# Partial sums of the middle stages: transfers that add in DRAM instead of load, add and store

## The reference

```python
lora_delta = lora_B @ lora_A * 0.5
normalized = (weight + lora_delta) / scale          # groups of 128
w_eff = codebook[searchsorted(thresholds, normalized)] * scale + lora_delta
h   = x @ w_eff.T                                   # 4096 x 2048
out = x_in + h @ W_base.T + b_base + 2 * mixture(h @ A_w.T, softmax(h @ router_w.T), cores) @ B_w.T
```

## Time and profile before

| | |
|---|---|
| median of 3 runs | 2330.87 us (2330.3 to 2331.73) |
| profiled execution: time, span | 2334.6 us, 2331.3 us |
| PE busy | 2252.6 us (97%) |
| DVE, ACT, POOL busy | 1952.5 (84%), 1495.4 (64%), 1391.5 us (60%) |
| HBM read, written | 306.41 MB, 151.13 MB |
| token part of stage 1, of stage 2 | about 891 to 1244 us, about 1427 to 1776 us |

### The profile page before, as it was taken

How to read it: one execution, slowest core, us unless ns; L and a number is a source line. 1 busy time by engine, 2 the same in 40 slices (tenths; PEclk the granted TensorE clock), 3 DMA queues, 4 the chain that set the end, 5 groups by cost and what they waited for, 6 DMA issues and landing times.

```text
span 2331.3 us, 31903 instructions
## 1 busy us (share of the span) xinstructions
PE 2252.6 (97%) x11610; PEld 2061.2 (88%) x11610; DVE 1952.5 (84%) x2501; ACT 1495.4 (64%) x1962; POOL 1391.5 (60%) x902
## 2 busy tenths in 40 slices
PE   3989899999999999999999999999999999999999
PEld 2445479999999989999999989999999999999998
DVE  8999998889988977989997988999996766777676
ACT  7999978989877764666664865666663664121221
POOL 6888846669874545878775635988872132233331
PEclk9999999999999999999999999999999999999999
DMA  6787854444334334656664334566656666656454
GB/s 209 260 288 272 315 208 170 163 170 145 133 128 149 116 109 169 254 214 240 248 231 153 115 109 167 221 244 246 234 223 195 187 193 192 226 192 235 189 222 154
DMA packets 133233, 459.62 MB, mean 197 GB/s; under 512 B 14114, under 2 KB 66914, under 8 KB 96354
## 3 DMA queue, kind: packets, MB, share of 16 engines
q1 hardware_dynamic: 133076, 457.59, 56.1%
HBM read 306.41 MB, written 151.13 MB: 196 GB/s over the span
## 4 chain that ended last, share of the span: by engine, by line
PE 80%; DVE 8%; DMA 4%; ACT 3%; POOL 2%; issue 2%; SPq 0%; DVEq 0%; POOLq 0%; ACTq 0%
PE m L1228 6%; PE m L1227 6%; PE m L1229 6%; PE m L1179 5%; PE m L1180 5%; PE m L1181 5%; DVE acc L1701 5%; PE m L1120 5%; PE m L1334 4%; PE m L1336 4%; PE m L1335 4%; PE m L1294 3%; PE m L1293 3%; PE m L1295 3%; PE m L1284 3%; PE m L1285 2%
## 5 line engine op out<-in xcount | busy, mean ns | idle before, releaser
L1701 DVE SCALAR_TENSOR_TENSOR acc<-mk,dj,acc 128x1024 f32<-128x1024 uint8 x736 | 944.4, 1283 | 91.4 <-ACT mk L1449 73.2
L1449 ACT ACTIVATE mk<-wr,bj 128x1024 uint8<-128x1024 f32 x736 | 811.1, 1139 | 0.5 <-DVE acc L1701 0.4
L2014 POOL TENSOR_TENSOR pp<-pp,tm 128x1024 f32<-128x1024 f32 x184 | 456.9, 2483 | 22.9 <-POOL tm L2000 1.5
L2000 POOL TENSOR_SCALAR tm<-mp,dj 128x1024 f32<-128x1024 uint8 x192 | 225.8, 1177 | 219.8 <-ACT mp L1455 213.0
L1799 DVE TENSOR_TENSOR kl<-kw,kh 128x416 fp32r<-128x416 f32 (+3 forms) x310 | 240.5, 785 | 84.5 <-ACT kh L1484 83.5
L1484 ACT ACTIVATE kh<-kw 128x416 fp32r<-128x416 f32 (+3 forms) x310 | 169.1, 548 | 183.2 <-DMA kw<-in_wb 91.9
L1228 PE MATMUL m<-gl,xh 128*128 128x384 f32 (+2 forms) x800 | 280.9, 351 | 0.0
L1227 PE MATMUL m<-gh,xh 128*128 128x384 f32 (+2 forms) x800 | 280.6, 351 | 0.0
L1229 PE MATMUL m<-gh,xl 128*128 128x384 f32 (+2 forms) x800 | 279.9, 350 | 0.0
L1455 ACT ACTIVATE mp<-wr,bj 128x1024 uint8<-128x1024 f32 x224 | 255.0, 1139 | 13.7 <-POOL wr L1980 13.7
L1761 DVE TENSOR_TENSOR part<-m,part 128x448 f32<-128x448 f32 (+4 forms) x362 | 210.8, 593 | 34.1 <-PE m L1229 16.7
(11 more groups left out here) (249 smaller groups left out, 5140.8 us busy)
## 6 DMA issues: line engine op xcount, KB each, us to landing
part<-part SPq DMA_DIRECT2D x191, 1036.0 KB, 4.8
rows<-in_wb SPq DMA_DIRECT2D x61, 1036.0 KB, 4.8
out<-part SPq DMA_DIRECT2D x31, 1024.0 KB, 4.8
kw<-in_ws SPq DMA_DIRECT2D x128, 208.0 KB, 2.7
xw<-in_x SPq DMA_DIRECT2D x96, 256.0 KB, 5.1
kw<-in_wb SPq DMA_DIRECT2D x92, 192.0 KB, 2.4
wr<-in_w SPq DMA_DIRECT2D x32, 512.0 KB, 5.8
dl<-delta SPq DMA_DIRECT2D x30, 512.0 KB, 5.4
```

What stands on the lines that cost most here:

```text
L1449: e.activation(R.mk[m % NM], w, ACT.Identity, bias=R.bj[:, j:j + 1], scale=GROW).then_inc(S["mk"], 1)
L1701: e.scalar_tensor_tensor(R.acc, R.mk[m % NM], R.dj[:, j:j + 1], R.acc, ALU.mult, ALU.add).then_inc(S["ac"], 1)
L2014: e.tensor_tensor(R.pp, first, R.tm[scaled_level(q, i)], ALU.add).then_inc(S["pp"], 1)
```

## The change

In stages 1 and 2 the part is no longer loaded. Each unit is evicted by a copy into the part buffer (products that come second add to the first in SBUF, as before), and the whole buffer is then added to `part` in DRAM by one transfer that POOL issues, `add_part`, with `accum_op=ALU.add` and each row of 2072 cut in two pieces of 1036. The evictions are divided: ACT copies the rests and the chunks 0 to 2 (`mul_copied`, semaphore `ea`), DVE the seven products and chunks 3 and 4 (`mul_evicted`, semaphore `ed`). The first write to a buffer waits for the transfer that added it three tokens before (new semaphores `pa`). The event `half_stored` stands after unit 10 of a mixed pair (6 of a pair of chunks) for its even token, `pair_stored` at unit 1 of the next pair for its odd token, and `close` for token 31. The transfer of a token in stage 2 waits for that of stage 1. SP keeps the x loads, the weight loads and the part stores of stage 0. The first ring pieces of the next weight part wait for `pa` instead of `po`.

```diff
...
@@ -221,3 +221,2 @@
                 yield ("x_split", g, 2 * p + 3)
-                yield ("more", g, p)
             if at == 4 and mixed(p + 1):
@@ -236,2 +235,6 @@
                 yield ("split", SPLITS[g + 1][at])
+        if at == (10 if mixed(p) else 6):
+            yield ("half_stored", g, p)
+        if p and at == 1:
+            yield ("pair_stored", g, p - 1)
         if at == (9 if mixed(p) else 5):
@@ -578,6 +581,20 @@
 PAIR_FIRST = {g: {p: min(k for k, u in enumerate(UNITS_OF[g]) if u[0] == p) for p in range(PAIRS)} for g in MIXED}
-MC_BASE, ED_BASE = [0, NCH * NT], [0, len(DVE_CHUNKS) * NT]
+
+
+def by_scalar(u):
+
+    return u[1] == "rest" or u[1] == "chunk" and u[3] in ACT_CHUNKS
+
+
+MC_BASE, EA_BASE, ED_BASE = [0, NCH * NT], [0, len(ACT_CHUNKS) * NT], [0, len(DVE_CHUNKS) * NT]
 for _g in MIXED:
+    scalar_units = sum(by_scalar(u) for u in UNITS_OF[_g])
     MC_BASE.append(MC_BASE[-1] + len(UNITS_OF[_g]))
-    ED_BASE.append(ED_BASE[-1] + len(UNITS_OF[_g]))
+    EA_BASE.append(EA_BASE[-1] + scalar_units)
+    ED_BASE.append(ED_BASE[-1] + len(UNITS_OF[_g]) - scalar_units)
+
+
+def token_units(g, t, scalar):
+
+    return [k for k, u in enumerate(UNITS_OF[g]) if u[0] == t // 2 and t % 2 in unit_tokens(u)[0] and by_scalar(u) == scalar]
 
...
@@ -602,4 +614,12 @@
 
-def added(g, k):
-    return ED_BASE[g] + k + 1
+def evicted(g, k):
+
+    scalar = by_scalar(UNITS_OF[g][k])
+    earlier = sum(by_scalar(u) == scalar for u in UNITS_OF[g][:k])
+    return ("ea", EA_BASE[g] + earlier + 1) if scalar else ("ed", ED_BASE[g] + earlier + 1)
+
+
+def wait_unit_evicted(e, S, g, k):
+    name, count = evicted(g, k)
+    e.wait_ge(S[name], count)
 
@@ -664,3 +684,3 @@
     if g in MIXED:
-        e.wait_ge(S["ed"], added(g, PAIR_FIRST[g][t // 2] + NCH * (t % 2) + c))
+        wait_unit_evicted(e, S, g, PAIR_FIRST[g][t // 2] + NCH * (t % 2) + c)
     elif c in ACT_CHUNKS:
@@ -864,3 +884,6 @@
             p = HOME[r]
-            e.wait_ge(S[f"po{p}"], 16 * (g * PER_SLOT[p] + (g == LAST and p == (NT - 1) % 3)))
+            if g == 1:
+                e.wait_ge(S[f"po{p}"], 16 * PER_SLOT[p])
+            else:
+                e.wait_ge(S[f"pa{p}"], 16 * (g - 1) * PER_SLOT[p])
         if g == LAST:
@@ -884,19 +907,6 @@
 
-    def load_part(g, t):
-        if t < 3:
-            e.wait_ge(S["used"], NS * (g - 1) + RELEASED[t])
-        else:
-            e.wait_ge(S[f"po{t % 3}"], slot_round(g, t - 3))
-        e.dma_start(R.part[t % 3], part[t]).then_inc(S[f"pi{t % 3}"], 16)
-
-    def store_part(g, t):
-        if g == 0:
-            for c in range(NCH):
-                wait_evacuated(e, S, g, t, c)
-        else:
-            e.wait_ge(S["ed"], added(g, last_unit(g, t, 0)))
-        if (g, t) == (LAST - 1, NT - 1):
-            e.dma_start(part[t][:, 0:HX], R.part[t % 3][:, 0:HX]).then_inc(S[f"po{t % 3}"], 16)
-        else:
-            e.dma_start(part[t], R.part[t % 3]).then_inc(S[f"po{t % 3}"], 16)
+    def store_part(t):
+        for c in range(NCH):
+            wait_evacuated(e, S, 0, t, c)
+        e.dma_start(part[t], R.part[t % 3]).then_inc(S[f"po{t % 3}"], 16)
 
...
@@ -1015,8 +1021,2 @@
                 load_x(g, 1)
-            if s == NS - 5:
-                load_part(g, 0)
-            if s == NS - 3:
-                load_part(g, 1)
-            if s == NS - 1:
-                load_part(g, 2)
         elif what == "chunk":
...
@@ -1038,14 +1038,4 @@
                 load_x(g, 2 * p + 3)
-            if p:
-                store_part(g, 2 * p - 1)
-        elif what == "more":
-            g, p = at
-            if p:
-                load_part(g, 2 * p + 2)
         elif what == "half_done":
-            g, p = at
-            store_part(g, 2 * p)
-            if p + 1 < PAIRS:
-                load_part(g, 2 * p + 3)
-            elif g == 1:
+            if at == (1, PAIRS - 1):
                 raw(2 * FIRST[LAST])
...
@@ -1523,2 +1513,15 @@
         e.activation(R.part[t % 3][:, cols(c)], R.m[c][:, 0:width(c)], ACT.Copy).then_inc(S["ea"], 1)
+
+    def mul_copied(g, k):
+        p, kind, u, i = UNITS_OF[g][k]
+        t = 2 * p + u
+        part, bank = R.part[t % 3], (*R.m, R.pd)[unit_bank(UNITS_OF[g][k])]
+        if t >= 3 and k == token_units(g, t, True)[0]:
+            e.wait_ge(S[f"pa{t % 3}"], slot_round(g - 1, t - 3))
+        e.wait_ge(S["mc"], multiplied(g, k))
+        if kind == "chunk":
+            to, of = part[:, cols(i)], bank[:, 0:width(i)]
+        else:
+            to, of = rest_columns(part, i), rest_bank(bank, i)
+        e.activation(to, of, ACT.Copy).then_inc(S["ea"], 1)
 
@@ -1626,2 +1629,6 @@
                 weight(g + 1, 1)
+        elif what == "mul":
+            g, k = at
+            if k and by_scalar(UNITS_OF[g][k - 1]):
+                mul_copied(g, k - 1)
         elif what == "next_rounded":
@@ -1742,3 +1749,3 @@
 
-    def mul_added(g, k):
+    def mul_evicted(g, k):
         p, kind, *at = UNITS_OF[g][k]
@@ -1746,16 +1753,15 @@
         part, bank = R.part[t % 3], (*R.m, R.pd)[unit_bank(UNITS_OF[g][k])]
-        if k == first_unit(g, t, 0):
-            e.wait_ge(S[f"pi{t % 3}"], slot_round(g - 1, t))
+        if t >= 3 and k == token_units(g, t, False)[0]:
+            e.wait_ge(S[f"pa{t % 3}"], slot_round(g - 1, t - 3))
         e.wait_ge(S["mc"], multiplied(g, k))
         if kind == "chunk":
-            c = at[1]
-            to, of = part[:, cols(c)], bank[:, 0:width(c)]
-        elif kind == "rest":
-            to, of = rest_columns(part, at[1]), rest_bank(bank, at[1])
-        else:
-            first = HX * TARGET[at[0]][1]
-            to, of = part[:, first:first + SW], bank[:, 0:SW]
-            before = target_before(g, k)
-            if before is not None:
-                e.wait_ge(S["ed"], added(g, before))
+            e.tensor_copy(part[:, cols(at[1])], bank[:, 0:width(at[1])]).then_inc(S["ed"], 1)
+            return
+        first = HX * TARGET[at[0]][1]
+        to, of = part[:, first:first + SW], bank[:, 0:SW]
+        before = target_before(g, k)
+        if before is None:
+            e.tensor_copy(to, of).then_inc(S["ed"], 1)
+            return
+        wait_unit_evicted(e, S, g, before)
         e.tensor_tensor(to, of, to, ALU.add).then_inc(S["ed"], 1)
...
@@ -2061,2 +2068,11 @@
         e.tensor_tensor(s4, a12, s2, ALU.subtract).then_inc(S["qs"], 1)
+
+    def add_part(g, t):
+        wait_unit_evicted(e, S, g, token_units(g, t, True)[-1])
+        wait_unit_evicted(e, S, g, token_units(g, t, False)[-1])
+        if g == 1:
+            e.wait_ge(S[f"po{t % 3}"], 16 * PER_SLOT[t % 3])
+        else:
+            e.wait_ge(S[f"pa{t % 3}"], slot_round(g - 2, t))
+        e.dma_start(part[t], R.part[t % 3], accum_op=ALU.add, max_dma_last_dim=4 * HX).then_inc(S[f"pa{t % 3}"], 16)
 
@@ -2163,3 +2179,9 @@
             token_sums(*at)
+        elif what == "half_stored":
+            add_part(at[0], 2 * at[1])
+        elif what == "pair_stored":
+            add_part(at[0], 2 * at[1] + 1)
         elif what == "close":
+            if at[0]:
+                add_part(at[0], NT - 1)
             if at[0] == 1:
...
```

More of the change, by code:

```diff
@@ L105 @@
     "sl", "lb0", "lb1", "lb2", "la0", "cb", "id", "la", "ds0", "ds1", "ds2", "dq0", "dq1", *(f"w{r}" for r in range(RAW)), "r0", "r1", "r2", "f2", "f3", "f5", "f6", "f7",
-    *(f"k{r}" for r in range(RING)), "x0", "x1", "x2", "x3", "pi0", "pi1", "pi2", "po0", "po1", "po2",
+    *(f"k{r}" for r in range(RING)), "x0", "x1", "x2", "x3", "pa0", "pa1", "pa2", "po0", "po1", "po2",
     *(f"pj{k}" for k in range(5)), *(f"ou{k}" for k in range(5)), "xs0", "xs1", "bw", "bb", "cr",
@@ L578 @@
 PAIR_FIRST = {g: {p: min(k for k, u in enumerate(UNITS_OF[g]) if u[0] == p) for p in range(PAIRS)} for g in MIXED}
-MC_BASE, ED_BASE = [0, NCH * NT], [0, len(DVE_CHUNKS) * NT]
+def by_scalar(u):
+    return u[1] == "rest" or u[1] == "chunk" and u[3] in ACT_CHUNKS
+MC_BASE, EA_BASE, ED_BASE = [0, NCH * NT], [0, len(ACT_CHUNKS) * NT], [0, len(DVE_CHUNKS) * NT]
 for _g in MIXED:
+    scalar_units = sum(by_scalar(u) for u in UNITS_OF[_g])
     MC_BASE.append(MC_BASE[-1] + len(UNITS_OF[_g]))
-    ED_BASE.append(ED_BASE[-1] + len(UNITS_OF[_g]))
+    EA_BASE.append(EA_BASE[-1] + scalar_units)
+    ED_BASE.append(ED_BASE[-1] + len(UNITS_OF[_g]) - scalar_units)
+def token_units(g, t, scalar):
+    return [k for k, u in enumerate(UNITS_OF[g]) if u[0] == t // 2 and t % 2 in unit_tokens(u)[0] and by_scalar(u) == scalar]
 def last_unit(g, t, reads):
     return max(k for k, u in enumerate(UNITS_OF[g]) if u[0] == t // 2 and t % 2 in unit_tokens(u)[reads])
-def first_unit(g, t, reads):
-    return min(k for k, u in enumerate(UNITS_OF[g]) if u[0] == t // 2 and t % 2 in unit_tokens(u)[reads])
 def prod_unit(g, p, n):
@@ L1001, in sync_program @@
             if g == LAST:
-                if s == 1:
-                    store_part(LAST - 1, NT - 1)
-                if s == 4:
```

(10 more changed lines are left out.)

8 lines of the change are left out of this document (4 added, 4 removed).

## The result

The changed kernel takes 2365.29 us (median of 4, 2364.13 to 2365.82) against 2330.59 us for the kernel before on the same chip: 1.0152 times as long, 95% interval 1.0139 to 1.0164. Forecast were 2328.0 us and a range from 2320 to 2350. The profiled execution took 2364.13 us with a span of 2362.3 us, 31.0 us above the span of before.

A forecast was written before the change was run, and what follows sets the result against it. PE bounds the two token stages, busy 343.72 of 348.35 us. Terms -4.8 - 1.0 + 2.5 + 0.5 = -2.8 us against the median of 2330.87 gave 2328.0 us, range 2320 to 2350.

The forecast's parts named there:

- The stage starts: Start of both token stages: DVE freed of the first two chunks' evictions, 1.0 us gained, between 0 and 2.3.
- POOL trails PE by about that much: Middle of stages: transfers' waits on evictions cost nothing more, as POOL runs about 5.9 us behind, read at 1085.17 us.
- 1.4 + 8 us plus POOL's trail of 5 is below 18: Middle of stages: issue, landing and trail fit the buffer's some 15 us plus 3 in the bank, so DVE doesn't wait.
- the booked -4.8: Middle of both stages: 4.8 of about 6 us of PE's losses gained as DVE's lateness goes, between 0 and 6.
- The term put at nothing: POOL's queue: 32 transfers a stage at 1.4 us fit its idle time, 20.0 of 21.2 us a pair, costing nothing.
- +2.5 and +0.5 us: Stage ends: later transfers delay next weights, 2.5 us lost at the first (0 to 8), 0.5 at the second (to 6).
- into an emptier queue: First stage's end: weight loads go out 5.1 us later but take 2.4 us, reaching ACT 0.8 us later than before.
- the rival of the slow transfer: Adding transfer of about 12 us or more costs at stage ends and in the middle: 2339 us, chance 0.13.
- POOL as the bound: Rival: from 2.0 us a transfer POOL is as long as PE in every pair; at 2.4, 2352 us; chance 0.26.
- the 7 us that I had worked out by it: Adding transfer's landing by the Skill page's halved rate: nearer 7 us than the 8 us taken.
- POOL locked out while it writes its pieces: Within the POOL-bound rival: each transfer waits one DVE level of 1.28 us, making 2.7 us a transfer.

The follow-up runs named there:

- all three moves: Changed kernel with second pair's first transfer ahead of normalising, token 29's transfer ahead of POOL's splits, three first-stage-end DVE splits one unit later: 2345.76 us.

## Why the prediction was wrong

**What held.** DVE 79.6% and ACT 75.7% in the 275 us (forecast 78 and 73), ACT's wait for x under 15 us, POOL at 88.8% (90 to 95 forecast) with 1.20 us a transfer (1.4 taken). The stage starts gave 1.09 us (1.0 booked). An x that is early and a DVE with room do remove stalls: with plain stores from SP stage 1's mixed pairs fall from 306.99 to 303.69 us. But stage 2's stay at 303.69 against 303.17, so the gain there is 2.8 us, not 4.8.

**The step that failed, in the middle.** "POOL trails PE by about that much" and "1.4 + 8 us plus POOL's trail of 5 is below 18". The trail was read at 1085 us, in a quiet pair. At the second pair it is 13 us: 942.5 against an eviction at about 930. 13 + 11.3 is above 18, and the booked -4.8 became +15.6 us; 10.7 of it went when that one transfer was moved. The trace of before has the place, in POOL's timeline; the prediction didn't look:

```profile
930.89 2.55 POOL L2038 TENSOR_TENSOR xl<-xw,xh 128x512 fp32r<-128x512 f32 x2
933.39 2.41 POOL L1972 TENSOR_TENSOR wr<-wr,dl 128x1024 f32<-128x1024 f32 x1
935.88 2.76 POOL L1980 TENSOR_TENSOR wr<-wr,rs 128x1024 f32<-128x1024 f32 x1
938.61 1.89 POOL L2019 TENSOR_TENSOR wr<-wr,sc 128x1024 f32<-128x1024 f32 x1
940.58 2.40 POOL L2026 TENSOR_TENSOR wr<-wr,dl 128x1024 f32<-128x1024 f32 x1
```

**The term put at nothing.** POOL's issuing was costed "at nothing, with a cover that is nearly used up". Plain stores from POOL take 12.7 us more than plain stores from SP, 8.2 of them in the mixed pairs: the queue costs without any adding. A part of this may be the cut of the rows, which the two kernels don't share. Which of POOL's instructions it delays outside the second pair wasn't followed.

**The step that failed, at the ends.** +2.5 and +0.5 us were booked, 5.86 and 12.03 measured. Three things were missing. The loads were said to go out "into an emptier queue" at 2.4 us each; the first took 5.8 beside token 30's transfer, and behind token 31's three took 6.7 to 8.1, where plain stores from POOL left 3.6 to 5.0. DVE's split of 6.90 us held up token 30's last copy; the earlier trace rows had POOL's splits, not what they do to DVE's. And at the second end only the first buffer was followed, not those of tokens 30 and 31.

**The adding transfer.** 9.4 us instead of 8, within the bounds of 4.8 to 16. Taken alone the size was nearly right, and the rival of the slow transfer (from 12 us on, 2339) did not come; nor did POOL as the bound (from 2.0 us on, 2352). Each rival asked when one cost alone would decide. What came was the sum of both against one and the same slack, with each below its own point. The Trainium skill, page "Collectives: The Full Stack", section "The bandwidth ceiling: the fold count and why AG ≠ RS ≠ AR", says that the second read halves the rate; it says it of the adding step of a collective. The time on the queue agrees, 15.8% against 7.5% for the same bytes; the landing, 9.4 against 5.2 us, is 1.8 times as long, above the 7 us that I had worked out by it. Half the rate over the whole 4.8 us of a plain transfer would have given 9.6 us, an estimate by that page, and near the measured 9.4.

**POOL locked out while it writes its pieces** did not show: 64 transfers took 1.165 to 1.652 us, less than one DVE level above the least.

**What stays open.** With all three moves the kernel is still 14.0 us above before by the medians, 10.7 by the spans of the profiled executions. By PE's phases 4.6 us lie in the mixed pairs of stage 2, 3.0 in the second weight slots, 4.5 in the last weights. What is left of the cost at the ends, and POOL's 8.2 us in the mixed pairs beyond the moved transfer, stay without a tested cause. A last pair on the old path (loaded and added by DVE) wasn't tried. No kernel here with the sums kept beats the one before, and the plain stores from SP, which leave the sums out, show what the relief brings with nothing added: 0.05 to 0.24%.

## What to carry to other kernels

The time that a buffer is away is the issuing engine's trail plus the transfer's length, and both have to be read at the place where the trail is longest, not in a quiet stretch. Two costs that share one slack have to be priced together, since each alone may fit: an engine in order that is late now and then is a poor place for a transfer that others wait for, and the longer the transfer, the more so. At the ends of a stage look at what leaves just ahead of the loads that the next stage starts with; and when order is repaired, look at what else slid with the move.
